# Moving GpSimd's small steps, the next queries' products, the values' repair and the row scores in a layer kernel

## What is computed

```
qk = einsum('bhqd,bhkd->bhqk', q, k) / sqrt(s)
p  = softmax(qk, axis=-1) * triu(ones((s, s)))
v  = where(isnan(v), 0.0, v)
x  = embedded + einsum('bhqk,bhkd->bhqd', p, v)
attn = (x - mu) * rsqrt(var + eps) * gamma + beta
x  = layernorm(embedded + attn)
h  = silu((x @ w1.T) * s1) * ((x @ w2.T) * s2)
h  = gelu((h @ h1.T) * t1);  h = gelu((h @ h2.T) * t2)
x  = layernorm(x + (h @ w3.T) * s3)
```

## Time and profile before

| | us |
|---|---|
| median of 3 runs | 1321.23 |
| lowest, highest | 1320.97, 1322.27 |
| the profiled execution | 1322.63 |
| its span in the profile | 1320.6 |

### The profile page before, as it was taken

How to read it: one execution, slowest core, us unless ns; L and a number is a source line. 1 busy time by engine, 2 the same in 40 slices (tenths; PEclk the granted TensorE clock), 3 DMA queues, 4 the chain that set the end, 5 groups by cost and what they waited for, 6 DMA issues and landing times.

```text
span 1320.6 us, 18260 instructions
## 1 busy us (share of the span) xinstructions
PE 1211.8 (92%) x7322; PEld 815.2 (62%) x7322; DVE 812.8 (62%) x1239; ACT 528.4 (40%) x698; POOL 575.2 (44%) x502
## 2 busy tenths in 40 slices
PE   4378999989999999998999999999999999999997
PEld 2144666647675576746666476754777466664886
DVE  5855486566755576566864667556775668655412
ACT  6775411554125531375115551165312751154311
POOL 5856432365225542365224552255422653245332
PEclk8578899999998999999999899989999999997999
DMA  9971433516234252245225063341523452341000
GB/s 328 277 179 44 159 66 66 122 26 191 65 82 97 81 142 63 54 98 169 60 61 130 18 191 66 76 103 52 154 63 72 98 164 60 66 106 26 1 0 16
DMA packets 55451, 128.48 MB, mean 97 GB/s; under 512 B 4032, under 2 KB 15680, under 8 KB 53312
## 3 DMA queue, kind: packets, MB, share of 16 engines
q1 hardware_dynamic: 51008, 115.44, 34.1%
q10 hardware_dynamic: 4352, 11.80, 2.8%
HBM read 88.95 MB, written 38.27 MB: 96 GB/s over the span
## 4 chain that ended last, share of the span: by engine, by line
PE 68%; issue 10%; POOL 9%; DVE 6%; DMA 4%; ACT 2%; SPq 1%; POOLq 0%; DVEq 0%; ACTq 0%
PE PS L977 45%; POOL diag_probs L437 6%; PE PS L862 5%; PE PS L894 5%; PE PS L831 4%; DVE neg_max L646 4%; PE PS L913 3%; PE PS L920 2%; DMA qk_rows<-qk_lo 2%; DMA stacks<-qk_rows 2%; POOL rstd L450 1%; PE PS L926 1%; PE PS L841 1%; ACT probsT L558 1%; PE PS L871 1%
## 5 line engine op out<-in xcount | busy, mean ns | idle before, releaser
L646 DVE TENSOR_REDUCE neg_max<-PS 128x2 f32<-128x1024 f32 x256 | 299.7, 1216 | 72.6 <-PE PS L862 72.6
L558 ACT ACTIVATE probsT<-PS 128x1024 f32<-128x1024 f32 x256 | 247.9, 1021 | 121.9 <-PE PS L894 121.9
L424 POOL TENSOR_TENSOR hidA_lo<-hidA_full,hidA_hi 128x512 fp32r<-128x512 f32 x128 | 165.0, 1289 | 265.2 <-DVE hidA_hi L793 194.6
L977 PE MATMUL PS<-hidA_hi,g 128*128 128x512 f32 x512 | 207.5, 405 | 0.0
L977 PE MATMUL PS<-hidC_hi,g 128*128 128x512 f32 x512 | 205.7, 402 | 0.0
L977 PE MATMUL PS<-hidA_lo,g 128*128 128x512 f32 x512 | 200.3, 391 | 0.0
L977 PE MATMUL PS<-hidC_lo,g 128*128 128x512 f32 x512 | 200.2, 391 | 0.0
L437 POOL TENSOR_TENSOR diag_probs<-probsT,mask 128x512 f32<-128x512 f32 x120 | 154.8, 1293 | 57.5 <-PE PS L977 31.0
L424 POOL TENSOR_TENSOR hidC_lo<-hidC_full,hidC_hi 128x512 fp32r<-128x512 f32 x64 | 82.2, 1284 | 218.8 <-DVE hidC_hi L793 218.8
L894 PE MATMUL PS<-stacks 66*128 66x512 f32 x512 | 162.3, 441 | 0.9 <-ACT probsT L558 0.4
L579 ACT ACTIVATE hidC_full<-PS,scales 128x512 f32<-128x512 f32 x64 | 44.1, 690 | 254.8 <-PE PS L977 254.8
(11 more groups left out here) (101 smaller groups left out, 1634.2 us busy)
## 6 DMA issues: line engine op xcount, KB each, us to landing
stacks<-qk_rows SPq DMA_DIRECT2D x64, 512.0 KB
stacks<-qk_rows SPq DMA_DIRECT2D x32, 1024.0 KB
qk_rows<-qk_hi SPq DMA_DIRECT2D x32, 512.0 KB, 3.7
qk_rows<-qk_lo SPq DMA_DIRECT2D x32, 512.0 KB, 5.3
xT_sb<-xT_dram SPq DMA_DIRECT2D x8, 512.0 KB, 4.1
raw_weights<-h1T_dram ACTq DMA_DIRECT2D x8, 512.0 KB, 10.4
raw_weights<-h2T_dram ACTq DMA_DIRECT2D x8, 512.0 KB, 9.1
x_tok<-x_dram SPq DMA_DIRECT2D x8, 512.0 KB, 5.5
```

The source lines that it names most:

```text
L424: nc.gpsimd.tensor_tensor(lo[:, m, :], full[:, m, :], hi[:, m, :], ALU.subtract).then_inc(lo_done, 1)
L558: nc.scalar.activation(PT[:, s % RING, 2 * pair:2 * pair + 2, :], PS[:, 2 * pair:2 * pair + 2, :], ACT.Exp, scale=SCALE).then_inc(exp_done, 1)
L646: nc.vector.tensor_reduce(NEGM[:, h // (H // 2), at:at + 2], PS[:, bank + 2 * side:bank + 2 * side + 2, :], AX.X, ALU.max, negate=True).th ...
L977: ins = nc.tensor.matmul(out, d if swapped else w, w if swapped else d, start=(k == 0 and part == 0), stop=(k == kts - 1 and part == 1))
```

## The change

Five things are changed; the arithmetic stays.

- **GpSimd's sums and roots.** X_AT becomes (5, 8, 12, 13), and the roots of block t move behind the masks of steps 6 + 4t and 7 + 4t. The first low half of the next queries comes ahead of the last block's first root, the second ahead of its second root.
- **Queries.** The four products of the next sample's queries leave `next_projections` and go between the last three parts of attention: one ahead of `values(14)`, two ahead of `values(15)`, one behind it. Of the values' products two tiles, not one, now stand behind the last transposes.
- **The last sample** has 4, 18 and 2 products of `keep_warm` where 8, 32 and 4 stood.
- **Values' repair.** The rows of the values' tile lie close together (272 each), and one pair of instructions over all 1024 columns, ahead of layer 2, takes the place of four pairs.
- **Row scores** stand six steps apart (4, 10, ..., 46 and 58, 64, ..., 100), the transposes of the maxima at steps 54 and 108.

```diff
-X_AT = (4, 7, 8, 11)
+X_AT = (5, 8, 12, 13)
...
-        UNIT_AT = {2 + 7 * u + 2 * (u // (UNITS // 2)): u for u in range(UNITS)}
-        TURN_AT = {58: 0, 116: 1}
+        UNIT_AT = {4 + 6 * u + 6 * (u // (UNITS // 2)): u for u in range(UNITS)}
+        TURN_AT = {54: 0, 108: 1}
...
-                    t, norm = divmod(s - (QT - 1 + LAG), QT)
+                    t, norm = divmod(s - (QT + LAG), QT)
...
+                if not last:
+                    split_qk(b + 1, range(0, 1))
                 rstd(b, QT - 1, 0)
                 if not last:
-                    split_qk(b + 1, range(0, 1))
+                    split_qk(b + 1, range(1, 2))
                 rstd(b, QT - 1, 1)
                 if not last:
-                    split_qk(b + 1, range(1, 2 * DT))
+                    split_qk(b + 1, range(2, 2 * DT))
...
+                if not last:
+                    guard_v(b + 1)
                 for layer, full, hi in ((2, hidC_full, hidC_hi), (3, hidA_full, hidA_hi)):
...
-                        if not last and layer == 2 and m < QT:
-                            guard_v(b + 1, m)
...
-                for s in range(STEPS - LAG, STEPS):
-                    values(b, s)
+                if b < B - 1:
+                    project_half(b + 1, 0, 0)
+                values(b, STEPS - 2)
+                if b < B - 1:
+                    project_half(b + 1, 0, 1)
+                    project_half(b + 1, 1, 0)
+                values(b, STEPS - 1)
+                if b < B - 1:
+                    project_half(b + 1, 1, 1)
...
-                    keep_warm(7, 8)
+                    keep_warm(7, 4)
...
-                    project_v(b + 1, range(QT - 1))
+                    project_v(b + 1, range(2))
...
-                    keep_warm(7, 32)
+                    keep_warm(7, 18)
...
-                    project_v(b + 1, range(QT - 1, QT))
+                    project_v(b + 1, range(2, QT))
...
-                    keep_warm(7, 4)
+                    keep_warm(7, 2)
```

More of the change, by code:

```diff
@@ L24 @@
 VW = HD + 1
-VX = 288
+VX = H * VW
 EPS = 1e-5
@@ L106, in build_program @@
     ST, ST_f = both("stacks", [P, 2, QUAD, 2, S])
-    VXT = place("v_ones", [P, QT, VX], F32)
+    VXT = place("v_ones", [P, QT * VX + HD], F32)
     X = place("x_tok", [P, QT, D], F32)
@@ L802, in _ @@
             take_v(0)
-            for t in range(QT):
-                guard_v(0, t)
+            guard_v(0)
             sum_squares(0)
@@ L819, in _, with project_half @@
         def _(pe):
+            def project_half(b, n, k):
+                if n == 0 and k == 0:
+                    after(pe, xT_in, b, 16, 16)
+                    after(pe, y_taken, b, QT, -QT)
+                if n == DT and k == 0:
+                    after(pe, exp_done, b, 2 * STEPS, 0)
+                w, c = (WQ, WK)[n // DT], n % DT
+                ins = nc.tensor.matmul(PS[:, bank_qk(n), :], w[:, k, c * P:(c + 1) * P], XT[:, k, :],
+                                       start=(k == 0), stop=(k == DT - 1))
+                if k == DT - 1:
+                    ins.then_inc(qk_proj, 1)
             def project(b, parts):
[L822 removed]
                 for n in parts:
[L825 to L829 removed]
                     for k in range(DT):
[L831 to L833 removed]
+                        project_half(b, n, k)
             def project_v(b, tiles):
@@ L908, in values @@
                 after(pe, diag_ready, b, STEPS, s + 1)
-                after(pe, v_ready, b, QT, QT)
+                after(pe, v_ready, b, 1, 1)
                 lo, hi = kt * P, (kt + 1) * P
@@ L1043, in attention @@
                     values(b, s - LAG)
-                for s in range(STEPS - LAG, STEPS):
-                    values(b, s)
+                if b < B - 1:
[7 more added lines that the diff above has]
+                    project_half(b + 1, 1, 1)
             def next_projections(b, last):
-                if not last:
-                    project(b + 1, range(DT))
-                else:
-                    keep_warm(7, 8)
+                if last:
+                    keep_warm(7, 4)
                 turn_x2(b, 0, last)
```

28 lines of the change are left out of this document (9 added, 19 removed).

## The result

| | before | after |
|---|---|---|
| median, same chip, 4 runs each (us) | 1321.75 | 1260.39 |
| lowest, highest | 1320.97, 1324.15 | 1257.06, 1263.22 |
| the profiled execution, its span | 1322.63, 1320.6 | 1263.22, 1261.1 |

The ratio is 0.9532, 95% interval 0.9504 to 0.956. The profiled execution of after is its slowest. I split the span's 59.5 us by stages; the middle column is the prediction's.

What follows compares the result with a forecast made beforehand. TensorE was taken as the bound, idle for GpSimd's masks and for stacks and partly at low clock; 43.0 + 9.2 + 2.0 + 5.7 + 1.5 + 2.7 = 64.1 us less than 1322.63 led to 1257 us, range 1248 to 1282.

Steps and rivals of the forecast that it cites:

- The bound and the idle time at step 5: TensorE bounds nearly everywhere; its wait ahead of `values(5)` for mask 5, behind GpSimd's sum, goes: 19 us over eight samples.
- The low clock goes with it: Attention, exponential 7 to 15: without the idle time at step 5 the low clock goes too, some 19 us.
- The rival that it stays, at 1279: Something other than the idle time at step 5 sets the low clock, which stays: 1279 us, chance 0.13.
- Exponential 7 to 15 in 19.1 us: Attention's last eight steps: 18.8 us plus 0.3 of small waits per sample, 43.0 us less over eight samples.
- the signs of being wrong: Masks 6 or 8 late by over 1 us, clock below 0.9 between steps 7 and 15, waits at over two units a sample.
- The rival of new waits by roots: GpSimd's roots delay masks, 0.4 us per block, and low clock returns in two samples: 12 us more, 1269; chance 0.14.
- Step 15 to the feed-forward: End of attention, samples 1 to 6: queries among the last values, 17.15 us each, 9.2 us less in all.
- Sample 0: Its end of attention, with TensorE's wait for its branch and low clock behind: 22.1 us for 24.11, 2.0 less (0 to 5).
- Row scores, repair, stacks: Feed-forwards: values repaired in one piece and row scores six steps apart bring 1.5 us, layer 2's vanished stack waits 2.7.
- the rival that they don't fit: Row scores six steps apart: a cast delays every unit, 14 units wait 0.4 us in 7 samples: 1290 us, chance 0.06.
- Unit 1: Layer 2's second row-score unit waits 0.8 us for maxima behind the repair; 0.1 if VectorE keeps the port shared with GpSimd.
- Slower by new idle time: Rival: new waits before the last transposes (1.1 us) and at unit 1 (0.8) lower the clock: 1331 us, chance 0.03.

## Why the prediction was right, and where not

- **The bound and the idle time at step 5.** Right, and the one with most in it: 39.8 us of waits for masks became 4.8, those of 1.84 to 2.61 us at step 5 all gone, and one number undoes it (some 32 us).
- **The low clock goes with it.** Right: 1.00 in eight of eight, and filling the idle time alone does the same. The rival that it stays, at 1279, is out. The split into 19 us of idle time at step 5 and 19 of low clock can't be read off as it stands: products take 24.6 us less and idle time 12.9, since at low clock the slower products had covered other waits (2.37 us idle in sample 2, 3.05 in sample 3).
- **Exponential 7 to 15 in 19.1 us.** This is the step that failed in size: 19.8 on average, 1.0 us of waits above the floor of 18.76 and not 0.3. I took the tokens' landing, 0.1 to 0.9 us behind exponential 7, from eight samples of one execution as its range; in the profiled execution after they landed 0.3 to 1.8 behind it, with the issue 5.03 us ahead of it in seven samples of both. Above the floor of 8 x 18.76 stand 8.4 us, where I had taken 2.4: 3.5 are `values(6)` in four samples, 3.6 are masks 8 and 12 behind second roots, 1.3 are products that take a little longer. The wait of 1.27 us in sample 6 is by itself one of the signs of being wrong that I had named, mask 6 late by over 1 us; the other two didn't come. The rival of new waits by roots holds in kind: masks 8 and 12 cost 0.45 us a sample where it had 1.2, and no low clock came of it. For mask 12 I had counted 0.9 us of slack; with it sample 3, which has no wait over 0.3, takes 19.23 and not 18.76. I counted VectorE's chain by its short durations; with GpSimd beside it x_tok takes 1.4 us for 0.4 or 0.5, as in the earlier trace rows at 454.77, at both of its steps.
- **Step 15 to the feed-forward.** 17.15 predicted, 17.14 to 17.15 measured, and the wait 1.3 for 1.1. But the text gave the gain to the queries. Most of it is the roots' place: 16.95 with GpSimd's order alone. The moved value tile cost more (0.52) than the queries gave (0.37). The masks were misread too: I had mask 14 done by E + 0.9 and mask 15 by E + 3.4, as no root held them, and the waits ahead of the last two values gone in any case. They are done at E + 2.2 and E + 4.2, as the last sum with beta stands just ahead of mask 14 and block 2's first root ahead of mask 15 (it changed places with the second root only), and without the queries TensorE waits 0.64 us for each. That the sum came out at 17.15 is in part luck.
- **Sample 0.** 4.3 us for 2.0 (0 to 5). The rise of the clock from 0.79 that I had counted comes with GpSimd's order alone (0.92, 22.2 us for the 22.1 forecast). What I had left out is the idle time that the queries fill ahead of the branch, 2.2 us. In three later runs this window held 1.00 and took 18.0 to 18.4 us, so some 1.5 us of it are chance.
- **Last sample.** 13.90 for 13.5, and 12.45 to 13.5 was given. Its clock didn't fall, which 13.5 had allowed for; TensorE waited 0.64 us for each of the last two masks instead, which 12.45 had put at nothing.
- **Row scores, repair, stacks.** The three waits for stacks in layer 2 went (2.5 us, 2.7 forecast). The 1.5 for row scores and repair came to 0.4 at most: the working gave 1, and TensorE waits 7.2 us for maxima in the feed-forwards where it waited 7.0. No unit but the second waits, so the rival that they don't fit is out.
- **Unit 1.** Waits 1.05 where 0.8 was taken from a range of 0.1 to 1.3: GpSimd's low half started ahead of the pair's second instruction (304.22 and 304.78). Beside the single-input L635 GpSimd's instruction took 1.67 us for 1.29, which the rows of 256 columns hadn't shown. The Trainium skill (GPSIMD Engine Reference, Key points) has contention with instructions in a 2-port perf mode besides those with two SBUF inputs, and this row agrees with it, if L635, with 0.69 us for 1024 columns, ran in such a mode, which no run here shows; but VectorE didn't keep the interface through both, so the wait of 0.1 that I had worked out didn't come.
- **Slower by new idle time.** The waits of 1.32 and 1.05 us that the change brings never had a low clock behind them.

The forecast of 1257 us lies 3.4 below the median, which is within the changed kernel's own spread of 1257.06 to 1263.22. In the profiled execution 59.5 us went for the 64.1 of the sum: 5.6 too many were put at exponential 7 to 15 and 1.3 at the feed-forwards, 2.3 too few at sample 0, so misses of different causes partly cancel.

## What to carry to other kernels

Look for the small instruction in a queue that waits for something rare, a DMA or another engine's chain, and ask what stands behind it: moving it one place behind the work that is due first was worth some 32 of the 61 us. Where an idle time has a drop of the granted clock behind it, count both: in the eight windows products took 24.6 us less and idle time 12.9. Take the spread of a DMA's landing from more than one execution before giving it a slack of under 1 us, and price each part of a change apart, as one part can spend what another brings.

## What the runs showed of the hardware

**Idle time and the clock.** In the thirteen profiled executions in which nothing was put into the wait, 25 windows from exponential 7 to 15 have TensorE idle for 1.53 to 3.51 us ahead of `values(5)` or `values(6)`, and 22 have a mean granted clock of 0.74 to 0.93; of 79 with at most 1.27 us none is below 1.00. At the end of the attention two waits follow each other closely, of about 0.9 or 0.6 and 1.72 us: in the three runs with the roots in their old place 9 of 21 such windows (samples 1 to 7) have 0.84 to 0.91. With warming products in the wait at step 5 all eight windows from exponential 7 to 15 were 1.00. The Trainium skill (TensorE: Matmul & The Clock Gate, Part 1) has the array's clock at one of two levels by recent activity, at moments not tied to the program. The traces agree in that the same wait of 2.04 us left the clock at 1.00 in sample 3 of before and at 0.80 in sample 7.

**VectorE beside GpSimd.** The repair's second instruction, with two inputs, stood still until GpSimd's ended, whatever its size: 16 columns 1.28 us, 256 columns 1.41, 1024 columns 2.19. The number of inputs isn't what decides: the single-input L685 over 256 columns takes 0.41 us alone and 1.34 to 1.38 beside a GpSimd instruction that runs already, ending 0.15 us behind it. The single-input L635 over 1024 columns began 0.16 us ahead of GpSimd's, took 0.69 us and lengthened GpSimd's from 1.29 to 1.67; over 256 columns (0.28 us) it left it at 1.28.
